# Head attention of a two-layer metaformer block: a chunk's output leaves PSUM by VectorE instead of ScalarE and GpSimd

## What is computed

```python
attn = jnp.einsum('bhsd,bhtd->bhst', q, k) * temperature[None]   # 8 heads, 4096 x 4096, d = 32
attn = jax.nn.softmax(attn, axis=-1)
out = jnp.einsum('bhst,bhtd->bhsd', attn, v)
```

## Time and profile before

| | before |
|---|---|
| median of 3 runs | 2578.47 us |
| the profiled execution | 2575.45 us |
| its span, first to last instruction | 2573.7 us |
| the loop over chunks | about 198 to 1326 us of the span |
| VectorE busy over the span | 2174.8 us, 85% |
| TensorE busy over the span | 2011.3 us, 78% |
| ScalarE, GpSimd busy over the span | 1674.1 us, 789.6 us |

### The profile page before, as it was taken

The page is one execution under the profiler, slowest core; times in us unless marked ns, Lnnn a source line. Parts: engine busy times, 40 slices in busy tenths (PEclk is TensorE's granted clock), DMA queues, the critical chain, the costliest instruction groups (busy, mean ns, idle before and its releaser), DMA issues. The chain is left out here.

```text
span 2573.7 us, 84276 instructions
## 1 busy us (share of the span) xinstructions
PE 2011.3 (78%) x28546; PEld 1511.0 (59%) x28547; DVE 2174.8 (85%) x3745; ACT 1674.1 (65%) x2530; POOL 789.6 (31%) x587
## 2 busy tenths in 40 slices
PE   4739999999999999999966158703598309999994
PEld 3316666666666666666645146501286209999993
DVE  4989999999999999999977747678798757777775
ACT  5439999999999999999965335403255535555551
POOL 2652212113222232422221734405111642222220
PEclk8869999999999999999987579955799559999996
DMA  2002323323323223223222434330000561111115
GB/s 78 0 19 77 89 69 87 87 70 87 83 74 87 77 79 89 72 83 89 70 79 81 146 107 116 109 139 3 0 0 26 171 217 49 51 48 47 49 46 202
DMA packets 284540, 202.95 MB, mean 79 GB/s; under 512 B 153632, under 2 KB 260208, under 8 KB 284208
## 3 DMA queue, kind: packets, MB, share of 16 engines
q1 hardware_dynamic: 271216, 164.16, 22.4%
q0 software_dynamic: 12960, 35.73, 3.7%
q10 hardware_dynamic: 288, 2.10, 0.2%
HBM read 69.05 MB, written 108.60 MB: 69 GB/s over the span
## 5 line engine op out<-in xcount | busy, mean ns | idle before, releaser
L583 DVE TENSOR_TENSOR plow<-prob 128x1024 f16<-128x1024 f32 (+1 forms) x1024 | 1127.2, 1172 | 3.7 <-ACT prob L494 3.7
L494 ACT ACTIVATE prob<-scores 128x1024 f32<-128x1024 f32 x1024 | 999.9, 1025 | 88.5 <-PE scores L626 58.4
L646 PEld LDWEIGHTS outp<-vs,prob 128*128 128x128 bf16 x7680 | 515.1, 98 | 280.2 <-issue 220.8
L646 PE MATMUL outp<-vs,prob 128*128 (+1 forms) x7680 | 603.6, 193 | 24.9 <-DVE plow L583 12.2
L626 PE MATMUL scores<-qT,kT 128*128 (+1 forms) x2048 | 610.7, 380 | 7.5 <-DMA kT<-shift_rows 2.7
L648 PE MATMUL outp<-vs,plow 128*128 (+1 forms) x7680 | 601.2, 193 | 0.0
L648 PEld LDWEIGHTS outp<-vs,plow 128*128 128x128 f16 x7680 | 502.8, 97 | 57.5
L439 POOL TENSOR_TENSOR osum<-osb 128x128 f32<-128x128 f32 x64 | 250.4, 3912 | 811.5 <-DVE rec L588 811.5
L1495 POOL DMA_INDIRECT expert_rows<-m1eyo,m1edest x71 | 107.6, 1516 | 315.4 <-DVE m1eyo L1467 285.4
L1366 PE MATMUL m1eph<-m1exT,m1ew1c 128*128 128x128 f16 x3408 | 203.0, 220 | 0.4 <-ACT m1exT L1403 0.4
L1366 PEld LDWEIGHTS m1eph<-m1exT,m1ew1c 128*128 128x128 f16 x3408 | 194.1, 98 | 1.1 <-ACT m1exT L1403 0.6
(11 more groups left out here) (375 smaller groups left out, 3325.9 us busy)
## 6 DMA issues: line engine op xcount, KB each, us to landing
sorted_rows<-zero SPq DMA_DIRECT2D x128, 522.0 KB, 4.7
m1dstg<-in_L_ffn_W_dram SPq DMA_DIRECT2D x32, 512.0 KB
staged<-qk SPq DMA_DIRECT2D x73, 128.0 KB, 2.4
m0exr<-sorted_rows SPq DMA_DIRECT2D x71, 130.5 KB
m1exr<-sorted_rows SPq DMA_DIRECT2D x71, 130.5 KB, 2.1
m0cgot<-expert_rows SPq DMA_DIRECT2D x8, 1024.0 KB, 5.6
m1cgot<-expert_rows SPq DMA_DIRECT2D x8, 1024.0 KB, 7.9
tok<-in_x_dram SPq DMA_DIRECT2D x4, 1024.0 KB, 9.5
```

The costliest lines, as they stand in the source:

```text
L494: act.activation(prob[g % PBUF][:, :], scores[g % 2][:, :], ACT.Exp, scale=1.0 / (QK_SCALE * QK_SCALE)).then_inc(prob_ready, 1)
L583: dve.tensor_tensor(l[:, 0:n], p[:, 0:n], high(p)[:, 0:n], ALU.subtract).then_inc(low_ready, 1)
L646: pe.matmul(to, high(prob[g % PBUF])[:, cols], v, start=(g == 0 and i == 0 and j == 0), stop=False, skip_group_check=True)
```

## The change

VectorE takes over the whole of the work on a finished chunk. After its `low` of group 3 it inverts the denominators straight out of PSUM, copies the low halves (`V_LO`) to `osb`, which now has 32 columns per row tile, waits for that copy, and adds the high halves, read from PSUM. After its `low` of group 4 it multiplies sum and inverse into the image. ScalarE's copy and GpSimd's loop are gone; `out_taken` now comes from VectorE's sum.

```diff
@@ gpsimd
-            def add_halves(c):
-                pool.wait_ge(rec_ready, c + 1)
-                pool.tensor_tensor(osum[:, :, :], osb[:, :, 0:DH], osb[:, :, DH:2 * DH], ALU.add).then_inc(sum_step, 1)
-            def divide(c):
-                pool.wait_ge(sum_step, c + 1)
...
-            with pool.Fori(0, HEADS * NCH) as c:
-                add_halves(c)
-                divide(c)
@@ scalar
-            def take_out(c, u):
-                act.wait_ge(prob_used, c * NGRP + NGRP + PBUF)
-                act.wait_ge(osb_used, c + 1)
-                act.activation(osb[:, :, :], outp[:, u, 0:SPT * VN].rearrange("p (j v) -> p j v", v=VN), ACT.Copy
-                               ).then_inc(out_taken, 1)
...
-                    if before and g == 3:
-                        take_out(c - 1, 1 - u)
@@ vector
-            def invert(c):
-                dve.wait_ge(out_taken, c + 3)
-                dve.reciprocal(rec[:, :], osb[:, :, 2 * DH]).then_inc(rec_ready, 1)
+            def take_out(c, u):
+                dve.wait_ge(prob_used, c * NGRP + NGRP + PBUF)
+                out = outp[:, u, 0:SPT * VN].rearrange("p (j v) -> p j v", v=VN)
+                dve.reciprocal(rec[:, :], out[:, :, 2 * DH]).then_inc(rec_ready, 1)
+                dve.tensor_copy(osb[:, :, :], out[:, :, V_LO]).then_inc(osb_used, 1)
+                dve.wait_ge(osb_used, c + 1)
+                dve.tensor_tensor(osum[:, :, :], osb[:, :, :], out[:, :, V_HI], ALU.add).then_inc(out_taken, 1)
+            def divide(c):
+                dve.wait_ge(rec_ready, c + 1)
+                dve.wait_ge(out_taken, c + 3)
+                image = aout[:, :, :].rearrange("p k (r h d) -> p (k r) h d", h=HEADS, d=DH)
+                dve.tensor_tensor(image[:, ds((c % NCH) * SPT, SPT), ds(c // NCH, 1), :].squeeze(2), osum[:, :, :],
+                                  rec[:, :].unsqueeze(2).broadcast_to([P, SPT, DH]), ALU.mult).then_inc(divided, 1)
...
-                    if before and g == 5:
-                        invert(c - 1)
+                    if before and g == 3:
+                        take_out(c - 1, 1 - u)
+                    if before and g == 4:
+                        divide(c - 1)
```

More of the change, by code:

```diff
@@ L388, in attention @@
         zero = sb("zero", [P, 1, RW], F32)
-        osb = sb("osb", [P, SPT, VN], F32)
+        osb = sb("osb", [P, SPT, DH], F32)
         rec = sb("rec", [P, SPT], F32)
@@ L405, in attention @@
         shift_ready = sem("shift_ready")
-        sum_step = sem("sum_step")
+        divided = sem("divided")
         shift_set = sem("shift_set")
@@ L461, in _ @@
             pool.wait_ge(zero_set, 2)
-            with pool.Fori(0, HEADS * NCH) as c:
-                add_halves(c)
-                divide(c)
-            pool.wait_ge(osb_used, HEADS * NCH + 1)
         @block.scalar
@@ L480, in take_turned, with step @@
                                ).then_inc(turned_taken, 1)
-            def take_out(c, u):
-                act.wait_ge(prob_used, c * NGRP + NGRP + PBUF)
-                act.wait_ge(osb_used, c + 1)
-                act.activation(osb[:, :, :], outp[:, u, 0:SPT * VN].rearrange("p (j v) -> p j v", v=VN), ACT.Copy
-                               ).then_inc(out_taken, 1)
-            def step(c, u, more, before=True):
+            def step(c, u, more):
                 for g in range(NGRP):
@@ L500, in step @@
                         take_turned(c + NCH, u)
[L502 to L507, removed]
+            pairs_of_chunks(act, step)
         @block.sync
@@ L600, in _, with step @@
             dve.wait_ge(placed_dve, 2 * NCH)
-            def step(c, before=True):
+            def step(c, u, before=True):
                 for g in range(NGRP):
                     low(c, g)
-                    if before and g == 5:
-                        invert(c - 1)
[L608 to L611, removed]
+                    if before and g == 3:
+                        take_out(c - 1, 1 - u)
+                    if before and g == 4:
+                        divide(c - 1)
+            step(0, 0, False)
+            with dve.Fori(0, HEADS * NCH // 2 - 1) as it:
+                for u in range(2):
+                    step(it * 2 + 1 + u, 1 - u)
+            step(HEADS * NCH - 1, 1)
+            take_out(HEADS * NCH - 1, 1)
+            divide(HEADS * NCH - 1)
+            dve.wait_ge(divided, HEADS * NCH)
         @block.tensor
```

## The result

| | before | after |
|---|---|---|
| median of 5 runs | 2578.47 us | 2589.90 us |
| range of the runs | 2574.83 to 2581.09 | 2586.94 to 2593.34 |
| the profiled execution | 2575.45 us | 2590.12 us |
| its span | 2573.7 us | 2588.4 us |

The ratio of after to before is 1.0045, 95% interval 1.003 to 1.006: slower by 0.45%, 11.4 us between the medians. The profiled pair differs by 14.7 us, a ratio of 1.0057, which lies inside that interval. Forecast were +15.1 us, 2593.6 us and a range of 2580 to 2608 us.

A forecast was written before the change was run, and what follows sets the result against it. VectorE's list was taken as the bound. GpSimd leaving -29.1, new instructions +46.6, `low` behind short instructions -1.0 and the end -1.4 made +15.1 us: 2593.6 us against the median, range 2580 to 2608.

The forecast's parts named there:

- GpSimd's two stretches: GpSimd's sum and product slow two `low` on VectorE; removing them saves 0.47 us a chunk, 29.1 us.
- inversion, now out of PSUM: Inversion on VectorE, moved from group 5 to group 3, stays at 0.09 us: change 0.
- copy with its wait: VectorE's copy of the low half out of PSUM, awaited by the sum: 0.32 us a chunk, bounds 0.25 and 0.42.
- sum: VectorE's sum with one PSUM input, 128 columns: 0.21 us a chunk, bounds 0.15 and 0.29.
- product: VectorE's product of the same size as its sum: 0.21 us a chunk, bounds 0.15 and 0.29.
- `low` behind a short instruction: On VectorE such a `low` starts 0.015 us nearer; two such places instead of one, -1.0 us in all.
- The bound: VectorE's list limits the loop: no idle time before `low`; TensorE needs 16.0 of 17.638 us a chunk, 1.6 to spare.
- The routing's pair: Routing's 64-column copy out of PSUM and waiting sum, starts 0.25 us apart; plus 0.067 for 64 more columns gave 0.32.
- Register arithmetic and PSUM: The product's two address instructions hide under group 4's half-size `low`, and PSUM adds no fixed price: both 0.
- A: Rival: VectorE's `low` stands still for GpSimd's whole sum and product, 0.86 us a chunk; faster, 2569.6 us; chance 0.07.
- B: Rival: VectorE's short instructions leave holes or PSUM access costs; 0.2 us more a chunk, 2606 us; chance 0.14.
- C: Rival: no difference within 0.2%; VectorE's three new instructions cost at most 0.58 us a chunk, 2581.7 us; chance 0.08.

The follow-up runs named there:

- the first experiment: GpSimd's sum and product left out of the kernel before, image filled with ones once; period 17.167 us, 2581.36 us, 26 us less than before on that chip.
- half the change: Against the kernel before, GpSimd leaves the loop, VectorE sums and divides from SBUF, ScalarE keeps its copy; median 2574.02 us against 2578.39, ratio 0.9983.
- one input instead of two: In the kernel before, GpSimd's sum became a copy of the high half, its product stayed; period 17.508 us, one run 2571.37 us.

## Why the prediction was right

Point by point, a chunk's terms. The measured ones are mean pitches of the traces before and after; the product's and the GpSimd term were also measured by leaving them out (0.205 and 0.471).

| term | forecast | measured |
|---|---|---|
| GpSimd's two stretches | -0.47 | -0.471 |
| inversion, now out of PSUM | 0 | +0.005 (0.093 against 0.088) |
| copy with its wait | +0.32 | +0.292 (slot 0.18, wait 0.11) |
| sum | +0.21 | +0.205 |
| product | +0.21 | +0.202 |
| `low` behind a short instruction | -0.015 | +0.022 |
| change of the period | +0.255 | +0.255 |
| period | 17.89 | 17.893 |
| the whole attention | +15.1 us | +15.1 us |

The mechanism is the forecast one: VectorE's list is the limit, GpSimd's stretch goes, three instructions come. That the sum agrees to 0.001 us is luck. Copy, sum and product were together 0.04 too dear, inversion and `low` together 0.04 too cheap, and the two cancel; each alone would have been worth 2.6 us at the end, well inside the range.

*The bound.* VectorE has no idle time before `low` in either kernel, and taking out or adding its instructions moved the period by their pitch each time, as long as ScalarE wasn't late. The terms add, within 0.03 us for what stands right behind the inversion. TensorE's need of 16.0 us leaves out the four `turned` matmuls of a chunk (L620, 17.4 us busy in 45 chunks), so its spare was nearer 1.2 than 1.6 us; nothing hung on it.

*The copy* was taken 0.03 too dear. The routing's pair, from which the price came, has no short instruction ahead of it. Here the copy stands right behind the inversion. Without the copy the sum stood there, and it too was 0.24 us long instead of 0.29 and 0.03 cheaper. That points to the place. But the price also took a two-input instruction's step of 0.067 us for 64 more columns of a copy, and no run has this copy in another place, so which of the two was wrong isn't shown.

*`low` behind a short instruction.* Before, the `low` behind the inversion came after a mean of 1.113 us. The prediction counted two such places for `low` in the changed kernel; there is none, since sum and product aren't short enough: behind them `low` has its plain pitch, 0.602 and 1.135. So the old gain of 0.022 was lost instead of doubled.

*Register arithmetic and PSUM.* Both were weighed and put at zero, and both are. The product starts 0.60 us behind the half-size `low`. The sum right behind the inversion costs 0.17 us when one input is in PSUM (no copy) and 0.18 when both are in SBUF (ScalarE keeps its copy). The 120 against 58 cycles of the Trainium skill (VectorE: DVE Perf Modes, the TRN2 errata) do not show in these pitches.

*The rivals.* A fell with the first experiment: 0.471 us a chunk came back and not 0.86. (The 0.74 from which it was to decide is 0.71 by the prediction's own terms, 44.2 us over 62 chunks.) B fell with the product's. C is out by its own terms, 0.70 us for the three new instructions where it allowed 0.58, and by the timed interval, which begins at 1.003 where C ended at 1.002. The medians differ by 11.4 us, the attention by 15.1; with runs that spread by 6 us these times can't tell the two apart.

## What to carry to other kernels

When one engine's list is the bound, write the price of a step as its pitch in that list, and close the count of a whole period before changing anything: here it gave 17.89 us and 17.893 came, with terms right to 0.04 us. A total that agrees is no proof of its terms: three times here (the forecast, half the change, one input instead of two) it agreed because errors cancelled or one odd chunk made up the rest. Look at single pitches and single periods too. Taking a reader off the other engine (GpSimd) is a gain of its own, separate from where its work goes; send the work to an engine that waits, even if it needs four instructions for one, and put each where the distance between producer and consumer is large. A result that is read by the next instruction of the same engine cost 0.11 us of waiting here: put one other instruction between.

## What the runs showed of the hardware that was not expected

- GpSimd stretches a two-input VectorE instruction by less than its own length: 0.27 us for a two-input sum (457 ns alone), 0.20 for a two-input product (399 ns), 0.10 for a one-input copy (289 ns), none for a memset (205 ns). GpSimd's own side is hit harder: 1355 ns is the median for the 457, and 11.0 us in 17 of 64 sums, while VectorE's `low` follow one another without a gap.
- Behind a four-column inversion the next instruction's pitch is 0.02 to 0.03 us shorter: full-size `low` 1.113 against 1.135, half-size 0.578 against 0.602, sum 0.17 against 0.205.
- ScalarE's scaled copy of 64 columns is 322 ns long on average, but four in a row with nothing to wait for are issued 0.20 us apart (0.93 us for all four), so four small ones cost 0.8 us where the one of 260 columns was 386 ns long.
